# Attention: 32x32 block turns on VectorE, value products in four row groups, plain fp32 scores

## The reference

```python
q = (query @ W_Query + B_Query).reshape(B, Lq, 16, 64)   # query = layernorm(x), 512 rows a batch
k = (key @ W_Key + B_Key).reshape(B, Lk, 16, 64)         # key = value = ctx_1024
v = (value @ W_Value + B_Value).reshape(B, Lk, 16, 64)
scores = jnp.einsum('bqhd,bkhd->bhqk', q, k) / 8
probs = jax.nn.softmax(scores, axis=-1)
out = jnp.einsum('bhqk,bkhd->bqhd', probs, v).reshape(B, Lq, 1024)
x = x + out @ W_Output + B_Output
```

## Time and profile before

| | us |
|---|---|
| median of three runs | 1845.82 (1845.01 to 1846.94) |
| span of the profiled execution | 1843.2 |
| attention, first to last exponential | 457.6 to 1638.2 |

### The profile page before, as it was taken

The page is one execution under the profiler, slowest core; times in us unless marked ns, Lnnn a source line. Parts: engine busy times, 40 slices in busy tenths (PEclk is TensorE's granted clock), DMA queues, the critical chain, the costliest instruction groups (busy, mean ns, idle before and its releaser), DMA issues. The chain is left out here.

```text
span 1843.2 us, 25796 instructions
## 1 busy us (share of the span) xinstructions
PE 1663.1 (90%) x8789; PEld 1128.1 (61%) x8789; DVE 1209.8 (66%) x2689; ACT 843.8 (46%) x1870; POOL 608.1 (33%) x730
## 2 busy tenths in 40 slices
PE   6569999996999999999999999999999999973584
PEld 4447777754666666666666666666666766642352
DVE  6445656532777777776776776776777677757761
ACT  3324343431555555555555555555555555531110
POOL 2143445430333323332332332333232323220375
PEclk9669999997999999999999999999999999985697
DMA  8100000003323232323232322222223223213254
GB/s 254 27 23 12 12 12 1 1 0 106 69 47 69 47 92 46 69 69 69 47 92 47 67 72 61 54 65 74 56 60 79 59 53 86 46 45 99 44 85 58
DMA packets 68961, 109.46 MB, mean 59 GB/s; under 512 B 18400, under 2 KB 50400, under 8 KB 68832
## 3 DMA queue, kind: packets, MB, share of 16 engines
q1 hardware_dynamic: 62688, 99.29, 22.1%
q0 software_dynamic: 6144, 8.52, 3.0%
HBM read 27.84 MB, written 12.85 MB: 22 GB/s over the span
## 5 line engine op out<-in xcount | busy, mean ns | idle before, releaser
L1128 POOL TENSOR_SCALAR at_Pr<-at_Pr,at_rinv 128x512 f32<-128x512 f32 x512 | 355.8, 695 | 841.2 <-DVE at_rinv L1158 841.2
L1093 ACT ACTIVATE at_Pr<-at_ps,at_nmax 128x512 f32<-128x512 f32 x512 | 352.2, 688 | 535.2 <-DVE at_nmax L1153 533.6
L1153 DVE TENSOR_REDUCE at_nmax<-at_ps 128x1 f32<-128x512 f32 x512 | 351.2, 686 | 154.0 <-PE at_ps L958 142.5
L958 PE MATMUL at_ps<-at_k,at_q 128*128 128x512 f32 x1024 | 420.7, 492 | 10.8 <-DMA at_k<-at_k_own 9.1
L969 PE MATMUL at_ps<-k_ident,at_Pr 128*128 128x128 f32 x2048 | 309.8, 274 | 4.5 <-POOL at_Pr L1128 4.5
L969 PEld LDWEIGHTS at_ps<-k_ident,at_Pr 128*128 128x128 f32 x2048 | 250.5, 140 | 90.2 <-POOL at_Pr L1128 27.7
L1165 DVE COPY at_PT<-at_ps 128x512 f32<-128x512 f32 x384 | 261.4, 681 | 0.0
L958 PEld LDWEIGHTS at_ps<-at_k,at_q 128*128 128x128 f32 x1024 | 174.6, 191 | 130.7 <-issue 121.2
L979 PE MATMUL at_ps<-at_PT,at_V 128*64 128x512 f32 x1024 | 235.4, 602 | 0.9 <-DVE at_PT L1165 0.9
L1158 DVE RECIPROCAL at_rinv<-at_rsum 128x1 f32<-128x1 f32 x512 | 83.3, 163 | 161.1 <-ACT at_Pr L1093 159.1
L979 PEld LDWEIGHTS at_ps<-at_PT,at_V 128*64 128x64 f32 x1024 | 68.1, 137 | 122.5 <-issue 121.4
(11 more groups left out here) (236 smaller groups left out, 1996.5 us busy)
## 6 DMA issues: line engine op xcount, KB each, us to landing
at_k<-at_k_own SPq DMA_DIRECT2D x256, 256.0 KB, 4.3
k_x<-in_x SPq DMA_DIRECT2D x8, 512.0 KB, 8.5
mg_ctx<-in_ctx SPq DMA_DIRECT2D x8, 512.0 KB, 8.7
mx_ctxn<-in_ctx SPq DMA_DIRECT2D x8, 512.0 KB, 3.8
rows<-m_ctxT SPq DMA_DIRECT2D x16, 256.0 KB, 2.6
out<-k_x SPq DMA_DIRECT2D x8, 512.0 KB, 3.5
r_w<-in_L_ffn_w SPq DMA_DIRECT2D x16, 256.0 KB, 5.5
mx_w<-in_L_ffn_w SPq DMA_DIRECT2D x2, 1024.0 KB, 10.0
```

What stands on the lines that cost most here:

```text
L958: ins = pe.matmul(ps[:, S_BANK + j % 2, :], q2[:, u % 2, h, q:q + P], k2[:, u % 2, h, part, :], start=part == 0, stop=part == 1)
L1093: act.activation(Pr[:, j % 4, :], ps[:, S_BANK + j % 2, :], ACT.Exp, bias=nmax[:, j % 4:j % 4 + 1], accum_out=rsum[:, j % 4:j % 4 + 1]).th ...
L1128: pool.tensor_scalar(Pr[:, n % 4, :], Pr[:, n % 4, :], rinv[:, n % 4:n % 4 + 1], 1.0, ALU.mult, ALU.mult).then_inc(s["pn"], 1)
L1153: dve.tensor_reduce(nmax[:, j % 4:j % 4 + 1], ps[:, S_BANK + j % 2, :], AX.X, ALU.max, negate=True).then_inc(s["nmax"], 1)
```

## The change

- **Turning.** TensorE no longer turns tiles. VectorE turns each scaled tile by one instruction that transposes every 32 x 32 block by itself (`dve.transpose`), from `Pr` into `blocks`. A block turn leaves query group g (32 of the 128 queries of a tile) in partitions 32g to 32g + 31, now with keys there: partitions 32g + r hold key 32n + r for block n, along the free dimension the queries of that group.
- **Value products.** So a product has 32 keys as rows, one of 16 key blocks, for one query group and head: `weigh_values` issues 16 x 4 x 2 = 128 matmuls of 32 rows, 64 output rows and 128 columns (four tiles of 32 queries), the four groups in four row groups of the array and four PSUM banks, the two heads in two column halves. They stand in two runs: 4 blocks at slot 2, 12 at slot 3.
- **Values spread.** Each row group needs all values in its own 32 partitions. SP stores V (256 KB) in a DRAM buffer `spread_v`, waits for it, and loads it four times, once into each group of partitions (`V4`).
- **Scores.** Plain fp32, no split: each head's 64 rows of q and k stand in its own half of the partitions, and `score(u, m)` issues one matmul a head, the two in two row halves of the array. The query and key remainders, `k_own`, `k2` and the DMA copies of keys go.
- **Order.** The loop is over four slots m instead of eight tiles; a slot has the two heads' tiles for one range of queries. Three banks take scores, one bank all projections, four the weighed values and the output. `Pr` has six buffers instead of four. Values are projected in their own unit (slot 2), weighed one unit later, and mapped to the output two units later (slots 0 and 1), so the loop runs over U + 2. The router's norm stages move to other units of the batch.

The diff, cut to its core (`...` marks what is left out: most removed lines, which stand in the functions above, renamed loop variables, the router's row stages, declarations):

```diff
     U = HP * B
-    NBL = 2 * TPB
+    SLOTS = TPB
+    TILES = 2 * SLOTS
+    QG = 4
+    QW = P // QG
+    KB = S // QW
+    PV_FIRST = KB // 4
+    S_RING, P_RING = 3, 6
...
-        q2 = sb("q2", [P, 2, 2, S], F32R)
-        k_own = sb("k_own", [P, 2, S], F32R)
-        k2 = sb("k2", [P, 2, 2, 2, S], F32R)
+        q = sb("q", [P, 2, S], F32)
+        k = sb("k", [P, 2, S], F32)
         V = sb("V", [P, 2, TPB, P], F32)
-        Pr = sb("Pr", [P, 4, S], F32)
-        PT = sb("PT", [P, 2, 2, TPB, S], F32)
+        V4 = sb("V4", [P, 2, QG, TPB, P], F32)
+        Pr = sb("Pr", [P, P_RING, S], F32)
+        blocks = sb("blocks", [P, 2, 2, KB, TPB, QW], F32)
         oT = sb("oT", [P, S], F32)
-        nmax = sb("nmax", [P, 4], F32)
-        rsum = sb("rsum", [P, 4], F32)
-        rinv = sb("rinv", [P, 4], F32)
+        nmax = sb("nmax", [P, P_RING], F32)
+        rsum = sb("rsum", [P, P_RING], F32)
+        rinv = sb("rinv", [P, P_RING], F32)
...
-        S_BANK, T_BANK, A_BANK, O_BANK, Y_BANK = 0, 2, 4, 6, 7
-        s = sems(ctx, nc, "at", "w scaled q_ps qh ql k_ps kh kl k2 v_ps V s_ps nmax exp rinv pn t_ps "
-                 "pt_v pt_a pv oT y_ps x gT stats mv ve rstd xn tx_ps xT l_ps lg")
+        S_BANK, A_BANK, O_BANK = 0, 3, 4
+        Y_AT = slice(P, P + D)
...
-        ON_ACT = (4, 5)
...
-        NORM, APPLY, TURN, GATE, LAST = 1, 2, 3, 4, B - 1
+        NORM, APPLY, TURN, GATE, LAST = 2, 3, 4, 6, B - 1
...
+                def spread_values(u):
+                    sp.wait_ge(s["V"], u + 1)
+                    wait_count(sp, s["V4"], 16 * QG * (u - 1))
+                    sp.dma_start(spread_v[u % 2], V[:, u % 2, :, :].rearrange("p t d -> p (t d)")
+                                 ).then_inc(s["v_out"], 16)
+                    sp.wait_ge(s["v_out"], 16 * (u + 1))
+                    wait_count(sp, s["pv"], u - 1)
+                    for g in range(QG):
+                        sp.dma_start(V4[QW * g:QW * g + QW, u % 2, :, :, :].rearrange("p c t d -> p c (t d)"),
+                                     spread_v[u % 2].rearrange("(c r) f -> r c f", r=QW)).then_inc(s["V4"], 16)
                 for u in range(U):
...
+                    spread_values(u)
...
-                        wait_count(pe, s["V"], u)
+                    if of == 0:
+                        wait_count(pe, s["V"], u - 1)
+                        for r in range(DC):
+                            if routed(u - 2, TURN + r) is not None:
+                                pe.wait_ge(s["xT"], DC * routed(u - 2, TURN + r) + r + 1)
+                        if routed(u - 2, GATE) is not None:
+                            pe.wait_ge(s["lg"], routed(u - 2, GATE) + 1)
                     else:
...
+                        pe.wait_ge(s["q"], u + 1)
...
-                    pe.wait_ge(s["ql"], u + 1)
+                    pe.wait_ge(s["k"], min(u + 2, U))
...
+                def score(u, m):
+                    n = TILES * u + 2 * m
+                    wait_count(pe, s["exp"], n - 1)
+                    if m == 0:
+                        pe.wait_ge(s["q"], u + 1)
+                        pe.wait_ge(s["k"], u + 1)
+                    for h in range(2):
+                        own = slice(AD * h, AD * h + AD)
+                        ins = pe.matmul(bank(n + h), q[own, u % 2, P * m:P * m + P], k[own, u % 2, :],
+                                        start=True, stop=True)
                     ins.then_inc(s["s_ps"], 1)
 
...
+                def weigh_values(u, first_block, last_block):
+                    if first_block == 0:
+                        pe.wait_ge(s["blocks"], TILES * (u + 1))
+                        pe.wait_ge(s["V4"], 16 * QG * (u + 1))
+                        wait_count(pe, s["x"], 2 * u)
+                    for n in range(first_block, last_block):
+                        for g in range(QG):
+                            own = slice(QW * g, QW * g + QW)
+                            for h in range(2):
+                                ins = pe.matmul(ps[AD * h:AD * h + AD, O_BANK + g, 0:P],
+                                                V4[own, u % 2, n % QG, n // QG, AD * h:AD * h + AD],
+                                                blocks[own, u % 2, h, n, :, :].rearrange("p j q -> p (j q)"),
+                                                start=n == 0, stop=n == KB - 1)
+                    if last_block == KB:
+                        ins.then_inc(s["pv"], 1)
...
-                        ins = pe.matmul(ps[:, Y_BANK - half, D * (t % 2):D * (t % 2) + D], oT[:, P * t:P * t + P],
+                        ins = pe.matmul(ps[:, O_BANK + t, Y_AT], oT[:, P * t:P * t + P],
...
+                for u in range(U + 2):
+                    for m in range(SLOTS):
                         if there(u):
...
+                            score(u, m)
+                        if m < 2 and there(u - 2):
+                            output(u - 2, m)
+                        if m < 2 and there(u + 1):
+                            project(u + 1, m)
+                        if m == 2 and there(u):
+                            project_values(u)
+                        if m == 3 and there(u):
+                            if any(routed(u, r) is not None for r in (TURN, TURN + 1, GATE)):
+                                pe.wait_ge(s["V"], u + 1)
+                            for d in range(DC):
+                                if routed(u, TURN + d) is not None:
+                                    turn_rows(routed(u, TURN + d), d)
                             if routed(u, GATE) is not None:
...
+                                map_gates(routed(u, GATE))
+                        if m == 2 and there(u - 1):
+                            weigh_values(u - 1, 0, PV_FIRST)
+                        if m == 3 and there(u - 1):
+                            weigh_values(u - 1, PV_FIRST, KB)
...
+                    act.activation(q[:, u % 2, :], ps[:, A_BANK, :], ACT.Identity, bias=b_s[:, 0, u % HP:u % HP + 1]
+                                   ).then_inc(s["q"], 1)
...
+                    act.activation(k[:, u % 2, :], ps[:, A_BANK, :], ACT.Identity, bias=b_s[:, 1, u % HP:u % HP + 1]
+                                   ).then_inc(s["k"], 1)
...
+                    wait_count(act, s["v_out"], 16 * (u - 1))
...
+                    wait_count(act, s["y_ps"], 2 * u)
+                    act.activation(oT[:, :].rearrange("p (j g q) -> p g j q", j=TPB, g=QG),
+                                   ps[:, O_BANK:O_BANK + QG, 0:P].rearrange("p g (j q) -> p g j q", j=TPB),
+                                   ACT.Identity, bias=b_s[:, 2, u % HP:u % HP + 1]).then_inc(s["oT"], 1)
...
+                def weights_of(u, m, h):
+                    n = TILES * u + 2 * m + h
+                    act.wait_ge(s["nmax"], n + 1)
+                    wait_count(act, s["blocks"], n - P_RING + 1)
+                    at = slice(n % P_RING, n % P_RING + 1)
+                    act.activation(Pr[:, n % P_RING, :], bank(n), ACT.Exp, bias=nmax[:, at],
+                                   accum_out=rsum[:, at]).then_inc(s["exp"], 1)
...
+                    for m in range(SLOTS):
+                        if m == 0 and there(u - 2):
+                            heads_out(u - 2)
                         if there(u):
...
+                            for h in range(2):
+                                weights_of(u, m, h)
...
+                def row_max(u, m, h):
+                    n = TILES * u + 2 * m + h
+                    dve.wait_ge(s["s_ps"], SLOTS * u + m + 1)
...
+                def row_sum(u, m, h):
+                    n = TILES * u + 2 * m + h
+                    at = slice(n % P_RING, n % P_RING + 1)
+                    dve.wait_ge(s["exp"], n + 1)
+                    dve.reciprocal(rinv[:, at], rsum[:, at]).then_inc(s["rinv"], 1)
+                def turn(u, m, h):
+                    n = TILES * u + 2 * m + h
+                    dve.wait_ge(s["pn"], n + 1)
+                    if m == 0 and h == 0:
+                        wait_count(dve, s["pv"], u - 1)
+                    dve.transpose(blocks[:, u % 2, h, :, m, :],
+                                  Pr[:, n % P_RING, :].rearrange("p (n q) -> p n q", n=KB)).then_inc(s["blocks"], 1)
...
+                for u in range(U + 2):
+                    for m in range(SLOTS):
                         if there(u):
...
+                            row_max(u, m, 0)
+                            row_max(u, m, 1)
+                            if m:
+                                turn(u, m - 1, 1)
+                        if m == 0 and there(u - 1):
+                            turn(u - 1, SLOTS - 1, 1)
+                        if there(u):
+                            row_sum(u, m, 0)
+                        if m < 2 and there(u - 2):
+                            add_out(u - 2, m)
+                        if routed(u, NORM) is not None:
+                            take_stats(routed(u, NORM), m)
```

(50 more changed lines are left out.)

235 lines of the change are left out of this document (52 added, 183 removed).

## The result

The changed kernel takes 1769.13 us, median of 4 runs (1767.52 to 1773.68), against 1845.41 (1844.63 to 1846.94) of the kernel before on the same chip: ratio 0.9589, 95% interval 0.9576 to 0.9603. It is faster, by 76 us; the forecast was 154 us (1692). So the gain came out at half of what was forecast. The time is inside the wide range (1625 to 1910) and outside the forecast's own (1625 to 1760).

What follows compares the result with a forecast made beforehand. TensorE's own work was taken to bound the kernel. Per unit 3.4 + 4.0 + 6.9 + 1.1 + 0.7 = 16.1 us against 18.5; 64 x -2.4 = -154 gives 1692 us, range 1625 to 1910, the forecast's own 1625 to 1760.

Steps and rivals of the forecast that it cites:

- tripled, still hidden on average: TensorE's instruction fetch: instructions grow from about 200 to 620 a unit, taken to add no time.
- the turn on VectorE at 0.68: Block turn of a scaled tile on VectorE: 0.68 us taken, bounds 0.5 and 1.36; TensorE saves 3.5 us a unit.
- rival D: VectorE's block turn costs double, 1.36 us, making the unit 20.5 us and the time about 1974; chance 7%.
- Value products, 4.0 us for all eight tiles: TensorE's value products per unit: all eight tiles overlap fully, 3.6 us, plus 0.4 for filling and emptying in two runs.
- A: Value products overlap only partly, some four to six of eight tiles at once; time about 1827 with five; chance 15%.
- C: Value products in strict order, only two tiles meeting: 14.3 us, unit 26.4, time 2350; chance 5%.
- Seven more switches at 0.1: TensorE's array shape switches rise from 2 to 9 a unit, adding 0.7 us, bounds 0.3 to 1.0.
- Rival B: Instruction starts limit value products: 0.027 us a load-and-stream pair, 7.3 us a unit, time 1903; chance 15%.
- VectorE's chain of 3.67 us a slot: VectorE's in-order work through a slot, about 15.1 us a unit with norm work, 1.0 under TensorE.
- The spread as hidden traffic: Storing V and loading it four times takes some 7 us plus issue, hidden with 9 us of margin.
- Rival E: TensorE idles at times and drops to 1.2 GHz, some 14 us more per full unit; 8% together with anything else.
- TensorE over 93% busy between 600 and 1400 us: Sign that the forecast holds in the attention stretch, with TensorE's waits for turned blocks or scores near zero.

Runs made afterwards that it cites:

- 1: Changed kernel with the spread's store and loads moving only 8 of 512 columns from the third unit on: 1735.91 us, ratio 0.9409 to the kernel before.
- 4: Changed kernel with the value products cut into 1 and 15 blocks instead of 4 and 12: 1806.77 us, ratio 0.9801 to the kernel before.
- 6: Changed kernel with 14 of 16 key blocks weighed for only 64 of 128 query columns, same instruction count: 1764.63 us.
- experiment 2: Changed kernel with products in 8 and 8 blocks, the next unit's values projected in halves, routed work put behind the products: 1713.17 us.
- 10: The kernel of experiment 2 with 14 of 16 blocks weighed for only 32 of 128 query columns: 1679.41 us.
- experiment 5: Changed kernel with only 8 of 16 key blocks weighed, 2 in slot 2 and 6 in slot 3: 1590.56 us.
- 3: Changed kernel with only the cut of the value products moved, 8 and 8 blocks instead of 4 and 12: 1716.71 us.
- 7: The kernel of experiment 2 with the products back at 4 and 12 blocks as in the changed kernel: 1747.31 us.

## Why the prediction was half right

**What failed** is one sentence, in which a term was put at nothing: "The whole run fetches 72 packets, 0.3% of the DMA time; tripled, still hidden on average." On average it is: 0.7% of DMA time. But a unit's 620 instructions do not come evenly. 384 stand in one run that TensorE would clear in 2.9 us, that is 256 in 1.9.

Of 150 blocks from first to last exponential in the changed kernel's trace, TensorE used up 34 in under 2.3 us. From the start of such a block to the start of the next it is 3.4 us in the median, half of them between 2.8 and 3.9, the least 1.9 and the most 5.5 (medians 3.2 to 3.5 in 1, 4 and 6). Another 24 blocks took 2.85 to 3.2 us to use, and behind 13 of these TensorE does not wait even 0.1 us. Of the 85 that took 3.6 us or more none is followed by a wait of over 0.64 us, and shape switches alone make 0.5. So a dense stretch gets a block per some 3.4 us, 27 ns for a load and its matmul. That is a median of a wide spread and no fixed rate; where the next block came after 1.9 us, I take it that it was in store already.

The Trainium skill ("Runtime: NRT & Kernel Launch", Instruction fetch mechanics) says that crossing a 16 KiB boundary is "mostly hidden". For the kernel before its trace agrees (up to the last exponential, no record of a value product starts over 0.48 us behind the last, where 0.44 is due); for dense runs the trace after does not, with 1.00 us lost a unit.

**The sum,** per unit: forecast 16.1; a plain unit 15.84, with the routed work (0.40 by experiment 2) 16.24. Measured 17.39. The breaks add 3.91-2.91 = 1.00; the last 0.15 is of the size of the time at the low clock (42 us, which costs at most 21, or 0.33 a unit, and partly falls into breaks). 64 x (17.39-16.1) = 83 us, and the profiled run, 1773.68, is 82 over the forecast.

**Point by point.**
- Turning off TensorE, and the turn on VectorE at 0.68: right, it takes 0.706; rival D (binds from 0.81) is out.
```profile
L1152 DVE STREAM_TRANSPOSE at_blocks<-at_Pr 128x512 f32<-128x512 f32 x512 | 361.3, 706 | 84.6 <-POOL at_Pr L1127 84.2
```
- Scores, 0.86 a pair of heads with 0.2 for two switches: right. A score starts at 1014.36, the next work at 1015.42, 1.06 later.
- Value products, 4.0 us for all eight tiles: right, the weakest step. 1.14+2.91 = 4.05 us from the first product of each run to the work behind it. Rivals A and C are out.
- Seven more switches at 0.1: right. In the median over the trace, 0.52 us from a score to the record behind it where 0.43 is due, 0.20 from a value projection to the first product where 0.11 is: 0.09 each.
- Rival B took 0.027 us a pair for a floor of starts. The floor is 0.010 to 0.011 (experiments 6 and 10), below the 0.0144 that 128 columns need, so it binds nothing here. The Trainium skill ("TensorE: Matmul & The Clock Gate", Wait — 56ns, not 53.3ns?) has starts never less than about 25 ns apart; across these tiles the runs show less. Some 27 ns a pair is also what the block supply gives over a dense stretch, but that B has the same figure is chance: the products take 1.14+3.91 = 5.05 us a unit, not 7.3.
- VectorE's chain of 3.67 us a slot: never reached; experiment 5 shows that it does not bind slot by slot.
- The spread as hidden traffic: right for its own landing and wrong for its side effect. It flies beside the dense run; a break, once there, grows from at most 1.9 to 3.7 us.
- Rival E had the clock as a cause. It is the smaller part: 42 us at the low level cost at most 21. In the changed kernel it is mostly an echo: all nine low stretches later than 467 us start in or within 2.5 us behind a wait of over 1.8 us at a block edge. In experiments 2, 3 and 7, with few or shorter breaks, they sum to 7 to 10 us. It also falls without breaks: 18 us in experiment 5, which has none, and 34 in 10, which has 6.8 us of them. No run takes the clock away and keeps the breaks.
- "TensorE over 93% busy between 600 and 1400 us": it was, 762 of 800 us are 95%, and the unit was 1.3 us too long all the same. The sign was too blunt for a wait that comes in breaks:
```profile
600.00:1400.00 800.00, 762.41 (x13902) 464.53 (x13903) 575.28 (x1261) 384.60 (x927) 253.77 (x370) 0.98 0.34 84
```
- "Wrong if a unit takes over 17.2 us": it took 17.4.

**Still open:** why a break with the spread beside it grows to 3.7 us. The packet's end stands 1.1 to 1.9 us ahead of the resumption in either case, so it is its start that is late. Before breaks of over 0.8 us the last packet starts 0.8 us (median) after TensorE began the block that it is using, and up to 3.0 us after; without the spread's bytes (1) also 0.8, and never over 1.3. No row shows when the packet was asked for, so whether it waited behind the spread's packets is open.

## What to carry to other kernels

When a change cuts matmuls into many small ones, count instructions per stretch, not only per run: here, behind 256 instructions (128 loads and 128 matmuls) that TensorE used up in some 2 us, the next 256 began only 3.4 us (median) after they had begun. A gap with "issue" as its releaser inside a list of ready instructions, at a fixed distance in instructions, is that wait. The cure is an order of the same instructions: put the slow, wide matmuls between the small ones. Equal runs made 1713 us of 1769, and 1717 by one constant alone.

## What the runs showed of the hardware

- Eight fp32 tiles of 32 x 64 run at once: records of 128 columns start 14.4 ns apart (experiment 2), of 64 columns 11.2 (6) and of 32 columns 10.2 (10).
- Where TensorE used up a block of 256 instructions in under 2.3 us, the next began 3.4 us after it had begun in the median (1.9 to 5.5, changed kernel), with packets of 1.0 to 1.2 us in flight (medians of the runs).
- Less work gave no time: with 14 of 16 blocks at half their columns the run stayed at 1765 us, since the breaks grew from 54 to 80 us and the time at the lower clock from 42 to 82.
